# A transformer block's slot schedule: one values product deferred by a slot, odd maxima in a second PSUM bank

## The chip, the cores and the metric

The kernel runs on one core of one Trainium2 chip. The metric is the device time of one execution in microseconds (us), smaller is better. Engines are named as the profile names them: PE (TensorE matmul), PEld (TensorE weight load), DVE (VectorE), ACT (ScalarE), POOL (GpSimd), SP (SyncE, which issues most DMAs).

## What is computed

64 sequences of 128 tokens with 128 features attend to 77 keys of a context each (16 heads of depth 8); then a router sends each token to two of eight experts. Cut to what matters:

```python
x = x + tanh(g_xattn[0]) * xattn(_layernorm(x), ctx, ctx, wq, wk, wv)   # 16 heads, softmax over 77 keys
x = x + tanh(g_ffn[0]) * ffn(_layernorm(x), Wr, br, W1, b1, W2, b2)
# ffn: logits = x @ Wr + br; the best two experts of each token, gates = softmax over those two
#      h = relu(x @ W1[e] + b1[e]); out = sum of gates * (h @ W2[e] + b2[e])
```

## The kernel before

The work is cut by sequence (b = 0 to 63) and by group of four sequences (g = 0 to 15). Every engine runs its own list of instructions in order, and the lists are written out by hand: a loop over slots t = 0 to 103 (`slot(t)` of each engine, with u = t // 4 and r = t % 4) in which different sequences stand at different stages. In slot t the maxima of the scores are taken for sequence mx = t - 8, the scores, exponentials and value products for sc = t - 13, and the turning back and the residual of the attention for ob = t - 14. Between engines only semaphores order the work.

The steps of one sequence, four times each (h = 0 to 3, four heads at a time):

- `max_scores(b, h)` (L472, matmul at L482): PE writes scores of all queries into a PSUM bank; `head_max(b, h)` (L1023, L1028) on DVE takes the negated maximum over keys. From the fifth sequence on all four use the one bank `max_scores`, so a product waits until the maximum before it is taken (L477 to L479).
- `scores(b, h)` (L494, L503): scores with the maxima already subtracted, into two banks by turns; waits for the exponential two steps back. `exp_scores` (L740, L744) on ACT makes `probs`.
- `values(b, h)` (L507, L517): `probs` times values, into the bank `bank_oT`; `values(b, 0)` also waits until the bank was copied out for the sequence before. After the fourth, `output_rows(b)` on ACT (L734, L738) copies the bank to `oT`.
- `turn_o` (L521, L530) on PE turns `oT` back; `heads_normed` (L1041) on DVE divides by the sum, `add_attention` and `stats2_of` follow.

By r, once for each group, come `project_k` (r 0, L442), `turn_x1` (r 1, L448), `project_q` (r 2, L453), `project_v` (r 3, L458), `turn_x2` (r 3, L468) and `route` (r 0, L541), which puts router products into columns of the maxima's bank, where `make_logits` on DVE (L1062, L1067) reads them; the third maximum of an r 0 slot waits for that read (L480). `turn_max` (L486, L491) turns the maxima of two sequences. The queries go from `project_q` over ACT (`q_high`, L756) and DVE (`q_low`, L1020) through DRAM (`store_q`, then `stack_q`, L361, on SP) and come back stacked; the first maximum of the group, at r 0 two slots later, waits for them.

38 quads (four expert tiles of 128 rows each) are placed in slots 43 to 50, 55 to 62, 67 to 73, 75 and from 78 on. A quad has `hidden_part(q, 0)` and `(q, 1)` (L569, L591 to L593) in its slot, each into the bank `hidden_p`, which `relu` on ACT (L801, L810) must have read before the next one writes it; `rows_out` (L596, L605 and L607) in the slot after into the bank `y`; and `outputs` (L815, L819), the copy of `y` by ACT. From slot 81 on 16 dense units follow.

PE's slot order before, for what the prediction follows: `turn_max`, S0, M0, project, `hidden_part(q, 0)`, S1, M1, `turn_o`, `route`, `rows_out(q-1, 0)`, V0, S2, M2, `rows_out(q-1, 1)`, `turn_x1` or `project_v`, V1, S3, M3, V2, `hidden_part(q, 1)`, `turn_x2`, V3. (S, M and V are scores, maxima and values of h.) ACT's: copy of the turned maxima, `output_rows`, exp 0, `k_high` or `q_high`, relu of the first half, exp 1, `outputs`, exp 2, `turned_x1` or `v_columns`, exp 3, relu of the second half, `turned_x2`.

Of the kernel before, what the change touches and what calls it, by code (L numbers as in the profile page):

```python
# [18 lines left out]
MAX_LAG = 8  # L19
# [10 lines left out]
def clip(n, top):  # L30
    return max(0, min(n, top))


def flamingo_kernel(nc, x, ctx_t, g_xattn, g_ffn, w_att_t, w_router, b_router, w1, b1, w2, b2, out):
# [39 lines left out]
    t = 0  # L74
# [28 lines left out]
    with ExitStack() as stack:  # L103
# [171 lines left out]
        def active(s):  # L275
            return 0 <= s < B

        def group_on(g):
            return 0 <= g < NG
# [148 lines left out]
        def _(pe):  # L428
# [224 lines left out]
            def slot(t):  # L653
                u, r = t // NB, t % NB
                mx, sc, ob = t - MAX_LAG, t - SCORE_LAG, t - OUT_LAG
                for q in quads_at(t):
                    name_weights(q)
                if r == 0 and group_on(u - 3):
# [3 lines left out]
                if active(sc):  # L662
                    scores(sc, 0)
                if active(mx):
                    max_scores(mx, 0)
                if r == 0 and group_on(u - 1):
                    project_k(u - 1)
                if r == 2 and group_on(u - 1):
                    project_q(u - 1)
                for n in dense_at(t):  # L670
                    dense_units(n)
                for q in quads_at(t):
                    hidden_part(q, 0)
                if active(sc):
                    scores(sc, 1)
                if active(mx):
                    max_scores(mx, 1)
                if active(ob):
                    turn_o(ob, t)
                if r == 0 and group_on(u - 5):  # L680
                    route(u - 5, t)
                for q in quads_at(t - 1):
                    rows_out(q, 0)
                if active(sc):
                    values(sc, 0)
                    scores(sc, 2)
                if active(mx):
                    max_scores(mx, 2)
                for q in quads_at(t - 1):
                    rows_out(q, 1)  # L690
# [4 lines left out]
                if active(sc):  # L695
                    values(sc, 1)
                    scores(sc, 3)
                if active(mx):
# [12 lines left out]
                if active(sc):  # L711
                    values(sc, 3)

# [6 lines left out]
        def _(act):  # L720
# [139 lines left out]
            def slot(t):  # L860
# [20 lines left out]
                if t in (16, 17, 18):  # L881
                    b2_part(t - 16)
                if r == 0 and group_on(u - 3):
                    turned_max(u - 3, 1)
                if r == 2 and group_on(u - 2):
                    turned_max(u - 2, 0)
                if active(ob):
                    output_rows(ob)
                for q in quads_at(t - 2):
                    store_y(q)  # L890
                for n in dense_at(t):
                    dense_relu(n)
                if active(sc):
                    exp_scores(sc, 0)
                if r == 0 and group_on(u - 1):
                    k_high(u - 1)
                if r == 2 and group_on(u - 1):
                    q_high(u - 1)
                for q in quads_at(t):
                    name_biases(q)  # L900
                    relu(q, 0)
                if active(sc):
                    exp_scores(sc, 1)
                for q in quads_at(t - 1):
                    outputs(q)
                if active(sc):
                    exp_scores(sc, 2)
                if r == 1 and group_on(u - 1):
# [40 lines left out]
        def _(dve):  # L949
# [283 lines left out]
            def slot(t):  # L1233
# [21 lines left out]
                if r == 0 and group_on(u - 5):  # L1255
                    make_logits(u - 5)
                if active(ob):
                    heads_normed(ob)
                if active(mx):
                    head_max(mx, 2)  # L1260
                if active(t):
                    mean_var1(t)
                if active(ob):
                    add_attention(ob)
                    stats2_of(ob)
# [192 lines left out]
```

## Time and profile before

| | |
|---|---|
| time, median of 3 runs | 645.9 us (645.79 to 646.98) |
| span of the profiled execution | 693.9 us |
| PE busy | 579.1 us (83%) |
| DVE busy | 374.7 us (54%) |
| ACT busy | 363.7 us (52%) |
| POOL busy | 265.3 us (38%) |
| granted TensorE clock, mean | 0.925 of 2.4 GHz |

The profiled execution is longer than the timed runs, so a sum of its durations is made against 693.9 us. PE's matmuls are pipelined: a row's duration runs to its modelled end, and the next matmul may start before that, so what a product takes of PE's time is read from one start to the next. In the timeline a row has start, duration, engine, line, operation, out<-in and, in brackets, PE's idle time before it and what ended it. In the view of windows the first figure is the length, then the busy time of each engine with its number of instructions, the granted clock (1.00 is 2.4 GHz, 0.50 is 1.2 GHz), and DMA. In the view of waits the figures are total us, number of waits, longest. In the chain a row has start, us and what.

### The profile page before, as it was taken

Reading aid. Unit: us, or ns where it says so; the run is one execution under the profiler, and the core shown is the slowest. Engines: PE = TensorE matmul, PEld = TensorE weight load, DVE = VectorE, ACT = ScalarE, POOL = GpSimd, SP = SyncE. Lnnn points to the kernel's source line nnn. Section 1 sums busy time; section 2 is a strip of 40 time slices with the busy share of each in tenths; the row PEclk is TensorE's granted clock in tenths of the full one; section 3 lists DMA queues with packets and bytes.
Section 4 is the critical chain, followed back from the end, with each engine's and each line's share of the span. In section 5 each row is a group of like instructions: output and inputs, shape, how many; then the busy total and the mean of one; then the engine's idle time right before and its main releaser. Section 6 shows DMA issues by size and latency. Waiting matters only on the chain.

```text
span 693.9 us, 18476 instructions
## 1 busy us (share of the span) xinstructions
PE 579.1 (83%) x6201; PEld 412.4 (59%) x6213; DVE 374.7 (54%) x1361; ACT 363.7 (52%) x835; POOL 265.3 (38%) x281
## 2 busy tenths in 40 slices
PE   2459998989787999899789899788886788899877
PEld 0225555555455566666467667466664587778656
DVE  4455876688655765445765554665543331242354
ACT  5216765655455466666456656455555345456222
POOL 6020010100554002443544435544455255566660
PEclk9968998988788899999999999899999689999999
DMA  4445644544433376664676654553332245764221
GB/s 116 118 115 148 159 107 126 137 105 119 142 95 112 73 118 104 148 103 138 104 132 115 147 109 139 97 125 83 97 107 81 70 98 136 133 148 128 77 77 49
DMA packets 158121, 78.65 MB, mean 113 GB/s; under 512 B 85088, under 2 KB 153312, under 8 KB 158032
## 3 DMA queue, kind: packets, MB, share of 16 engines
q1 hardware_dynamic: 119760, 45.65, 30.4%
q0 software_dynamic: 7168, 14.69, 8.9%
q10 hardware_dynamic: 31104, 17.13, 8.9%
q8 instruction: 54, 0.88, 0.5%
q14 instruction: 35, 0.29, 0.2%
HBM read 30.72 MB, written 36.75 MB: 97 GB/s over the span
## 4 chain that ended last, share of the span: by engine, by line
PE 65%; issue 9%; DMA 7%; DVE 7%; ACT 7%; another core or an unknown queue 2%; POOL 1%; ACTq 1%; SPq 1%; DVEq 0%; POOLq 0%
PE y L607 11%; PE bank_oT L517 9%; PE scores L503 8%; PE max_scores L482 5%; DMA q_st<-q_dram 4%; PE hidden_p L591 4%; PE o L530 3%; PE hidden_p L592 3%; PE hidden_p L593 3%; DVE neg_max L1028 3%; ACT probs L744 2%; PE max_scores L541 2%; PE bank_oT L648 2%; ACT hidden L810 2%
## 5 line engine op out<-in xcount | busy, mean ns | idle before, releaser
L1028 DVE TENSOR_REDUCE neg_max<-max_scores 128x4 f32<-128x308 f32 x244 | 116.2, 476 | 158.7 <-PE max_scores L482 149.4
L744 ACT ACTIVATE probs<-scores 77x512 f32<-77x512 f32 x256 | 148.8, 596 | 69.9 <-PE scores L503 64.2
L1351 POOL DMA_INDIRECT xs_dram<-rows,at x112 | 110.1, 983 | 92.6 <-PE max_scores L482 57.4
L1366 POOL DMA_INDIRECT back<-ys_dram,at x112 | 107.8, 963 | 90.4 <-PE max_scores L482 35.9
L517 PE MATMUL bank_oT<-probs,v_cols 77*9 77x128 f32 x2048 | 110.0, 291 | 13.6 <-ACT probs L744 8.6
L503 PE MATMUL scores<-q_st,k_st 128*77 128x128 bf16 x1024 | 111.7, 236 | 0.1
L482 PE MATMUL max_scores<-k_st,q_st 128*128 128x308 bf16 x244 | 78.8, 323 | 34.9 <-DVE neg_max L1028 12.3
L503 PEld LDWEIGHTS scores<-q_st,k_st 128*77 128x77 bf16 x1024 | 76.5, 124 | 50.8 <-issue 43.7
L810 ACT ACTIVATE hidden<-hidden_p,b_cols 128x128 f32<-128x128 f32 x256 | 73.5, 369 | 54.3 <-PE hidden_p L593 43.3
L607 PE MATMUL y<-w_sb,hidden 128*128 x608 | 96.8, 299 | 0.0
L607 PEld LDWEIGHTS y<-w_sb,hidden 128*128 128x128 f32 x608 | 84.7, 201 | 2.7
L517 PEld LDWEIGHTS bank_oT<-probs,v_cols 77*9 77x9 f32 x2048 | 30.8, 89 | 59.8 <-issue 28.1
L591 PE MATMUL hidden_p<-xsT,w_sb 128*128 128x128 bf16 x256 | 53.5, 228 | 15.2 <-ACT hidden L810 10.7
L819 ACT COPY ys<-y 128x512 f32<-128x512 f32 x38 | 22.3, 588 | 82.1 <-PE y L607 66.0
L1312 POOL TENSOR_TENSOR rstd<-ve,power 128x4 f32<-128x4 f32 x16 | 17.7, 1107 | 114.2 <-DVE ve L996 114.2
L1306 POOL TENSOR_TENSOR rstd<-ve,power 128x4 f32<-128x4 f32 x16 | 16.4, 1027 | 113.3 <-DVE ve L969 90.8
L593 PE MATMUL hidden_p<-xsT,w_sb 128*128 128x128 bf16 x256 | 52.7, 222 | 0.3 <-issue 0.3
L592 PE MATMUL hidden_p<-xsT,w_lo 128*128 128x128 bf16 x256 | 52.6, 222 | 0.0
L482 PEld LDWEIGHTS max_scores<-k_st,q_st 128*128 128x128 bf16 x244 | 25.1, 103 | 45.6 <-DVE neg_max L1028 20.8
L738 ACT COPY oT<-bank_oT 128x512 f32<-128x512 f32 x64 | 37.6, 587 | 22.2 <-PE bank_oT L517 15.1
L530 PE MATMUL o<-ident,oT 128*128 128x128 f32 x256 | 43.2, 296 | 5.9 <-ACT oT L738 5.9
L591 PEld LDWEIGHTS hidden_p<-xsT,w_sb 128*128 x256 | 25.2, 99 | 32.1 <-issue 27.4
(144 smaller groups left out, 931.9 us busy)
## 6 DMA issues: line engine op xcount, KB each, us to landing
ys_dram<-ys ACTq DMA_DIRECT2D x38, 256.0 KB
q_st<-q_dram SPq DMA_DIRECT2D x16, 512.0 KB
k_st<-k_dram SPq DMA_DIRECT2D x64, 77.0 KB
xs_all<-x SPq DMA_DIRECT2D x16, 256.0 KB, 4.2
q_dram<-q_hl SPq DMA_DIRECT2D x16, 256.0 KB
xs_dram<-zeros_b ACTq DMA_DIRECT2D x16, 256.0 KB, 3.5
out<-xs_all SPq DMA_DIRECT2D x16, 256.0 KB
k_dram<-k_hl SPq DMA_DIRECT2D x48, 77.0 KB
```

The source lines that it names most:

```text
L482: mm(max_to(b, h)[:, 0:PER * KEYS], q_st[g % 3][:, h, seq_cut(b, S)], k_st[g % 3][:, h, b % NB, :, :].rearrange("p j k -> p (j k)"), start ...
L503: last = mm(score_bank[h % 2][0:KEYS, j * S:(j + 1) * S], k_st[g % 3][:, h, b % NB, j, :], q_st[g % 3][:, h, seq_cut(b, S)], start=True, s ...
L517: last = mm(oT_bank[ROWS * j:ROWS * j + VW, h * S:(h + 1) * S], v_cols[g % 3][:, b % NB, h * PER + j, :], probs[h][:, j * S:(j + 1) * S], ...
L591: mm(o, w_hi[:, at_w], tiles[:, 0, cut], start=True, stop=False, skip_group_check=True)
L592: mm(o, w1_lo[:, at_w], tiles[:, 0, cut], start=False, stop=False, skip_group_check=True)
L593: last = mm(o, w_hi[:, at_w], tiles[:, 1, cut], start=False, stop=True, skip_group_check=True)
L607: last = mm(o, hidden[:, (2 * q + t // 2) % 4, t % 2, m, :], w2_sb[:, bass.ds(w + m * 128, 128)], start=False, stop=(m == HC - 1), skip_gr ...
L744: nc.scalar.activation(probs[h][:], score_bank[h % 2][0:KEYS, :], ACT.Exp, scale=SCALE).then_inc(s_exp, 1)
L810: last = nc.scalar.activation(hidden[:, k % 4, i, m, :], of[:, j * 128:(j + 1) * 128], ACT.Relu, bias=b1_cols[:, bass.ds(held[q][2 * half ...
L1028: V.tensor_reduce(neg_max[:, i // 2, :, h, i % 2], max_to(b, h)[:, 0:PER * KEYS].rearrange("p (j k) -> p j k", j=PER), AXIS_X, ALU.max, ne ...
L1351: G.indirect_dma_start(out=xs_dram[c % 2], out_offset=bass.IndirectOffsetOnAxis(ap=at[k][c % 4][:, i:i + 1], axis=0), in_=rows[c % 2][:, i ...
L1366: G.indirect_dma_start(out=back[k][:, b % 16, :], out_offset=None, in_=ys_dram[c % 2][0:TILES[c] * 128, :], in_offset=bass.IndirectOffsetO ...
```

## The change

Three things. First, the fourth values product V3 moves from the end of its slot to the next slot, behind S0, M0 and S1 of the next sequence; `output_rows` and `turned_max` on ACT move behind exp 0, and `turn_o` behind V0. Second, the order of the rest: projections behind V3 and `turn_max`, M1 ahead of `hidden_part(q, 0)`, S2 ahead of `route` and M2 right behind it, S3 ahead of V1, `turn_x1` and `project_v` behind V1; ACT takes exp 1 ahead of the first relu and exp 2 ahead of `outputs`; DVE takes `heads_normed` behind the third maximum. Third, in slots without a quad the odd maxima (h = 1 and 3, from the fifth sequence on) go to the bank `hidden_p`, so an even and an odd maximum no longer wait for one another; waits keep the bank between maxima and quads.

```diff
+        def lent(b, h):
+            return h % 2 == 1 and b >= NB and not quads_at(b + MAX_LAG)
         def max_to(b, h):
-            return (max_bank, score_bank[0], score_bank[1], y_bank)[h] if b < NB else max_bank
+            if b < NB:
+                return (max_bank, score_bank[0], score_bank[1], y_bank)[h]
+            return hidden_bank if lent(b, h) else max_bank
+        def max_before(b, h):   # number of the maximum last taken in the same bank
...
 # max_scores
-                n = HG * b + h + 1 - (HG if b < NB else 1)
-                if n > 0:
-                    pe.wait_ge(s_max, n)
+                if max_before(b, h) > 0:
+                    pe.wait_ge(s_max, max_before(b, h))
+                if lent(b, h) and quads_before(b + MAX_LAG):
+                    pe.wait_ge(s_relu, 2 * quads_before(b + MAX_LAG))
 # hidden_part
+                if half == 0 and lent_before(QUAD_AT[q]):
+                    pe.wait_ge(s_max, lent_before(QUAD_AT[q]))
 # PE's slot, the order after
+ scores(sc, 0); max_scores(mx, 0); scores(sc, 1); values(ob, 3); turn_max; project_k or project_q;
+ max_scores(mx, 1); dense_units; hidden_part(q, 0); scores(sc, 2); route; max_scores(mx, 2);
+ values(sc, 0); turn_o(ob); rows_out(q-1, 0); scores(sc, 3); values(sc, 1); turn_x1 or project_v;
+ rows_out(q-1, 1); max_scores(mx, 3); values(sc, 2); dense_out; hidden_part(q, 1); turn_x2; ranks
 # ACT's slot, the order after
+ exp 0; store_y; output_rows(ob); turned_max; k_high or q_high; dense_relu; exp 1; relu(q, 0);
+ exp 2; outputs(q-1); turned_x1 or v_columns; exp 3; relu(q, 1); rows_high, turned_x2
 # DVE's slot
-                if active(ob):
-                    heads_normed(ob)
                 head_max(mx, 2); mean_var1(t)
+                if active(ob):
+                    heads_normed(ob)
```

(The orders of PE and ACT are written here as lists; the diff has them as moved blocks.)

## Rows read from the trace of the kernel before

**Rows 1.** The page: span, and the chain that ended last, shares by engine.
```profile
span 693.9 us, 18476 instructions
...
PE 65%; issue 9%; DMA 7%; DVE 7%; ACT 7%; another core or an unknown queue 2%; POOL 1%; ACTq 1%; SPq 1%; DVEq 0%; POOLq 0%
```

**Rows 2.** Windows by stage: early attention, quads, and the end.
```profile
57.74:115.76 58.02, 52.58 (x676) 32.49 (x674) 43.06 (x159) 40.38 (x76) 5.05 (x5) 1.00 0.53 142
116.62:182.00 65.38, 58.48 (x651) 35.77 (x648) 50.76 (x190) 36.39 (x70) 9.31 (x9) 0.85 0.46 117
182.00:243.04 61.04, 50.49 (x517) 31.66 (x516) 37.67 (x142) 29.16 (x57) 24.59 (x25) 0.78 0.40 105
243.04:317.96 74.92, 68.75 (x845) 51.84 (x841) 38.96 (x142) 47.37 (x124) 24.77 (x25) 1.00 0.66 123
455.57:534.70 79.13, 69.17 (x872) 51.71 (x869) 41.03 (x153) 46.24 (x121) 37.33 (x38) 0.99 0.37 94
534.70:693.90 159.20, 132.04 (x1120) 110.65 (x1128) 51.74 (x184) 66.56 (x174) 81.13 (x84) 0.92 0.43 102
```

**Rows 3.** Waits of PE: first two rows from 48.95:182, the others from 243.04:534.70.
```profile
PE max_scores L482 <- DVE neg_max L1028: 5.8, 15, 0.9
PE max_scores L482 <- DMA q_st<-q_dram: 1.9, 4, 1.1
...
PE hidden_p L591 <- ACT hidden L810: 7.5, 11, 1.2
...
PE bank_oT L517 <- ACT probs L744: 6.2, 17, 0.5
PE group L442 <- ACT xT L777: 4.1, 4, 1.1
```

**Rows 4.** Timeline of ACT and PE in a slot with a quad.
```profile
297.13 0.59 ACT L819 COPY ys<-y 128x512 f32<-128x512 f32 x1 [3.34 <-PE y L607]
297.61 1.08 ACT L744 ACTIVATE probs<-scores 77x512 f32<-77x512 f32 x2
...
298.26 0.41 PE L517 MATMUL bank_oT<-probs,v_cols 77*9 77x128 f32 x8 [0.35 <-ACT probs L744]
```

**Rows 5.** Timeline of PE in a slot without a quad, r 1.
```profile
93.76 0.29 PE L482 MATMUL max_scores<-k_st,q_st 128*128 128x308 bf16 x1
93.89 0.39 PE L503 MATMUL scores<-q_st,k_st 128*77 128x128 bf16 x4
94.63 0.30 PE L482 MATMUL max_scores<-k_st,q_st 128*128 128x308 bf16 x1 [0.35 <-DVE neg_max L1028]
...
98.34 0.41 PE L517 MATMUL bank_oT<-probs,v_cols 77*9 77x128 f32 x8 [0.22 <-ACT probs L744]
98.68 0.24 PE L491 MATMUL o<-ident_b,nm_hl 128*64 128x128 bf16 x1
```

**Rows 6.** Timeline around the router's products, r 0: PE, then DVE.
```profile
89.96 1.03 PE L541 MATMUL max_scores<-wr_sb,xT 128*128 128x8 f32 x8 [0.46 <-issue]
...
91.03 0.19 DVE L1067 TENSOR_TENSOR logits<-max_scores,br_sb 128x32 f32<-128x32 f32 x1 [0.79 <-PE max_scores L541]
```

**Rows 7.** Chain of waits, 98 to 112 us: the way of the queries.
```profile
99.40 0.86 PE group L453 x2
...
102.17 2.70 DMA q_dram<-q_hl
...
104.89 5.85 DMA q_st<-q_dram
...
110.78 0.32 PE max_scores L482
```

**Rows 8.** Windows: four slots, one r 1 slot of them, a later r 1 slot.
```profile
87.26:109.30 22.04, 20.05 (x256) 12.46 (x255) 16.71 (x62) 14.53 (x29) 2.02 (x3) 1.00 0.52 137
...
93.51:98.85 5.34, 4.60 (x65) 2.76 (x62) 4.42 (x18) 3.34 (x6) 0.07 (x1) 1.00 0.52 116
...
116.62:123.93 7.31, 6.95 (x66) 4.35 (x62) 4.51 (x18) 3.51 (x6) 0.08 (x1) 0.59 0.49 94
```

More of the change, by code:

```diff
@@ L292, in ranks_before, with lent_before @@
             return len([c for c in range(NC) if RANKED[c] < s])
+        def lent(b, h):
+            return h % 2 == 1 and b >= NB and not quads_at(b + MAX_LAG)
         def max_to(b, h):
-            return (max_bank, score_bank[0], score_bank[1], y_bank)[h] if b < NB else max_bank
+            if b < NB:
+                return (max_bank, score_bank[0], score_bank[1], y_bank)[h]
+            return hidden_bank if lent(b, h) else max_bank
+        def max_before(b, h):
+            if b < NB:
+                return HG * (b - 1) + h + 1
+            n = HG * b + h - 1
+            while n >= HG * NB and lent(n // HG, n % HG) != lent(b, h):
+                n -= 1
+            if n >= HG * NB:
+                return n + 1
+            return 0 if lent(b, h) else HG * (NB - 1) + 1
+        def lent_before(s):
+            return max([HG * b + h + 1 for b in range(clip(s - MAX_LAG, B)) for h in range(HG) if lent(b, h)], default=0)
         def dense_before(s):
@@ L657, in slot @@
                     name_weights(q)
+                if active(sc):
+                    scores(sc, 0)
+                if active(mx):
+                    max_scores(mx, 0)
+                if active(sc):
+                    scores(sc, 1)
+                if active(ob):
+                    values(ob, 3)
                 if r == 0 and group_on(u - 3):
@@ L661, in slot @@
                     turn_max(u - 2, 0)
[L662 to L665, printed above, removed]
                 if r == 0 and group_on(u - 1):
@@ L669, in slot @@
                     project_q(u - 1)
+                if active(mx):
+                    max_scores(mx, 1)
                 for n in dense_at(t):
@@ L674, in slot @@
                 if active(sc):
-                    scores(sc, 1)
+                    scores(sc, 2)
+                if r == 0 and group_on(u - 5):
+                    route(u - 5, t)
                 if active(mx):
-                    max_scores(mx, 1)
+                    max_scores(mx, 2)
+                if active(sc):
+                    values(sc, 0)
                 if active(ob):
                     turn_o(ob, t)
-                if r == 0 and group_on(u - 5):
-                    route(u - 5, t)
                 for q in quads_at(t - 1):
@@ L684, in slot @@
                 if active(sc):
[L685 to L690, printed above, removed]
+                    scores(sc, 3)
+                    values(sc, 1)
                 if r == 1 and group_on(u - 1):
@@ L694, in slot @@
                     project_v(u - 1)
-                if active(sc):
-                    values(sc, 1)
-                    scores(sc, 3)
+                for q in quads_at(t - 1):
+                    rows_out(q, 1)
                 if active(mx):
@@ L710, in slot @@
                         ranks(c)
-                if active(sc):
-                    values(sc, 3)
             pe.wait_ge(s_wa, 16)
@@ L882, in slot @@
                     b2_part(t - 16)
+                if active(sc):
+                    exp_scores(sc, 0)
+                for q in quads_at(t - 2):
+                    store_y(q)
+                if active(ob):
+                    output_rows(ob)
                 if r == 0 and group_on(u - 3):
@@ L886, in slot @@
                     turned_max(u - 2, 0)
-                if active(ob):
[L888 to L894, printed above, removed]
                 if r == 0 and group_on(u - 1):
@@ L898, in slot @@
                     q_high(u - 1)
+                for n in dense_at(t):
+                    dense_relu(n)
+                if active(sc):
+                    exp_scores(sc, 1)
                 for q in quads_at(t):
@@ L902, in slot @@
                 if active(sc):
-                    exp_scores(sc, 1)
+                    exp_scores(sc, 2)
                 for q in quads_at(t - 1):
                     outputs(q)
-                if active(sc):
-                    exp_scores(sc, 2)
                 if r == 1 and group_on(u - 1):
@@ L1262, in slot @@
                     mean_var1(t)
+                if active(ob):
+                    heads_normed(ob)
                 if active(ob):
```

1 line of the change is left out of this document (removed).

## The prediction

> **What bounds the kernel now.** I read the page first, then windows by stage, then PE's waits, then single slots. The chain that ended last lies on PE for 65% of the 693.9 us, with 9% "issue" (PE waiting for nothing that the profile shows) and only 7% each on DMA, DVE and ACT [rows 1]. The windows by stage say that this PE is nearly full wherever quads run: 68.75 of 74.92 us at full clock, 69.17 of 79.13 us in the last quad stage [rows 2]. From 534.7 us on no attention runs, every moved call is inactive there, and the relative order of what is left on each engine stays: these 159.2 us [rows 2] are not touched. The change can act on about 486 us of slots, through PE's idle time, through what PE redoes at half clock, and through nothing else: it adds no product and removes none.
>
> There are three kinds of slot. In slots with a quad PE's holes are `hidden_part` waiting for the relu of the half before (7.5 us, 11 waits), a values product waiting for its exponential (6.2 us, 17) and `project_k` waiting for `turned_x2` (4.1 us, 4) [rows 3]. In early slots without a quad the holes are maxima waiting for DVE (5.8 us in 15 waits) and, at r 0, the first maximum waiting for the stacked queries (1.9 us in 4) [rows 3]. In late slots without a quad, 182 to 243 us, PE is busy 50.49 of 61.04 us and the granted clock is 0.78 [rows 2]: half clock costs there more than any one wait.
>
> **Small prices, from start to start at full clock.** S is 93.51 to 93.76, 0.25 us; M 93.76 to 93.89, 0.13; V 98.34 to 98.68, 0.34; `turn_max` 98.68 to 98.85, 0.17 [rows 5, 8].
>
> **Slots with a quad: values.** V2 waits 0.35 us in the shown slot because ACT takes `outputs` first, which itself waits for `rows_out` (3.34 us idle), and only then exp 2 and exp 3 [rows 4]. After the change exp 2 stands ahead of `outputs`, so V2 has its input long before; V3, whose exponential now sits behind `outputs`, is a slot later, behind S0, M0 and S1. Of the 6.2 us I take 5.0 (bounds 0 and 6.2; most of the 17 waits are of this kind).
>
> **Slots with a quad: the hidden bank.** After the second hidden part PE now has S0, M0, S1, V3, M1 ahead of the next first hidden part; before it had V3, S0, M0. The relu's end does not move, so the hole is filled by S1 + M1 = 0.38 us: 11 waits by 0.38 is 4.2 us; the last slots have no maxima, there it is 0.25. I take 4.0 (bounds 2.8 and 4.2). M1 must now wait for the first maximum, one DVE round behind M0, but S1 and V3 (0.59 us) stand between, and the relu that PE waits for ends later still.
>
> **Slots with a quad: `project_k`.** It waits for the end of an ACT queue that is not reordered there. Only S1 moves ahead of the hole: 4 x 0.25 = 1.0 us gained.
>
> **A new wait behind the router.** M2 now follows `route` directly, and at r 0 it waits until `make_logits` has read the bank. The router's products end at 90.99, DVE reads them from 91.03 to 91.22 [rows 6]; before, V0 and S2 (0.59 us) lay there and hid it. V0, `turn_o` and all behind M2 wait with it. That is about 0.3 us (bounds 0 and 0.35) in each r 0 slot that has both: 7 of them from slot 43 on, 2.1 us lost.
>
> **Slots without a quad.** With two banks M1 no longer waits for a DVE round (0.35 us in the shown r 1 slot) and V3's 0.22 us goes [rows 5]. Of four slots' 22.04 us PE is idle 1.99 [rows 8]; 0.46 of it is before the router's products, which still wait for the second maximum [rows 6]. Against the gain stand new waits, which the trace does not show and which I bound by a walk along both queues. V3 now comes after S1, exp 0 precedes `output_rows` on ACT, so V0 waits for a copy that starts some 1.1 us into the slot (0 to 0.2 us at r 1 and r 3). `turn_x1` and `project_v` move behind V1, their ACT copies stand ahead of exp 3, and S1 of the next slot and V3 wait for exp 3: 0 to 0.4 us. `turn_x2` has only M3 and V2 (0.47 us) between it and `project_v`, whose copy of 0.6 us it waits for: 0 to 0.36 us. Together up to 1.5 us in four slots, as much as can be gained. From slot 43 on there are two such fours: I take 2.0 us for the banks less 1.5 for the new waits, 0.5 gained. Slots 35 to 42: another 0.5. `heads_normed` moves behind the third maximum at no cost: `turn_o` is later too, DVE is busy 4.42 of 5.34 us [rows 8], and what follows it (`add_attention`, the second layer norm) has slots of slack.
>
> **The queries' way.** From `project_q` (ends 100.26) over ACT, DVE and two DMAs of 2.70 and 5.85 us the first maximum starts at 110.78 [rows 7]. It was late there: PE waited up to 1.1 us [rows 3]. The change puts S1, V3 and `turn_max` (0.76 us) between M0 and `project_q`. In the period from M0 of one group to M0 of the next the DMA way stays as it is and the rest gets 0.76 us longer, plus 0.3 behind the router, less the removed waits (0.35 + 0.22 and the like in two slots). I take +0.2 us for each of the five groups of slots 13 to 34, 1.0 us lost (bounds -0.5 and +4.0). `store_max` stands ahead of `store_q` in SP's queue, and its input is now two ACT copies later (two take 1.08 us [rows 4]); but `turn_max` and its copy still precede `project_q` and `q_high` on both engines, so SP has it issued first. `project_k` is later by the same 0.76 us; its stacked keys are needed a whole group later.
>
> **Sum.** -5.0 - 4.0 - 1.0 + 2.1 - 1.0 + 1.0 = -7.9 us of 693.9, 1.14%. The timed median is 645.9, 0.931 of the profiled span; I scale the sum by that: -7.4, **638.5 us**. With each bound taken on its side it runs from 632 (-14.4 us) to 648 (+2.7 us).
>
> **Rivals.**
>
> *The clock follows (B).* Between 116.6 and 243 us the clock is 0.85 and 0.78 [rows 2], which is 19.6 and 26.9 us at 1.2 GHz. An r 1 slot that is mostly at 1.2 GHz (0.59 on the mean, 6.0 of its us) takes 7.31 instead of 5.34 us [rows 8]: 0.33 us for each us at the low level, 15 us in all. If half of it goes because PE stands still less often, 7.6 us more come off: 631. All of it: 624. For it: the low stretches lie only in slots without a quad. Against it: from 57.7 to 115.8 us PE is idle 9% in the same short holes and the clock is 1.00 [rows 2], so short holes are not what brought it down. The Trainium skill (TensorE: Matmul & The Clock Gate, "A second HAM failure mode: psum-queue depth-cycling") says that cycling through PSUM banks makes PE idle briefly between groups so often that the clock swings between its levels; by that rule the second bank would give this rival. The trace of 57.7 to 115.8 us disagrees.
>
> *The queries' wait grows and takes the clock (D), slower.* Slots 16 to 44 have eight first maxima that wait for stacked queries. Filled holes elsewhere do not shorten the DMA way; they only bring PE to M0 sooner, where it then stands in one piece, some 2 us instead of up to 1.1. After the group with the 1.1 us wait (M0 at 110.78) the clock was low in the next slot [rows 7, 8], for the first time since 57.7 us [rows 2]. Price: 8 x 0.76 = 6.1 us, and 1.97 us for each added low stretch (7.31 - 5.34). With four of them it is 14.0 us against the 8.4 gained from slot 43 on: +5.6 us, scaled 651; it turns to slower from the second added stretch on. The Trainium skill (the same page, "HAM oscillation — how this bites in real kernels") says that bursts of products with a DMA wait between them start each burst at the low clock; by that rule it would be so here. The trace bears it out once for sure, so this is no small case.
>
> *Round trips only change their place (C).* The new waits of 1.5 us in four slots and behind the router come at their upper bounds, and in quad slots ACT (47.37 of 74.92 us busy [rows 2]) gives exp 3 and the relus back what exp 2 gained: about 645.5.
>
> **How the numbers follow.** The forecast has 0.46, B 0.18, C 0.13, D 0.23. The range from 624 to 652 holds B with all of its clock and D with four stretches. About 0.2% (1.3 us) is what a measurement of this kernel can tell from no change. Faster is the forecast and B, 0.64; same is C, 0.13; slower is D, 0.23.
>
> **What would show it.** Right: in the quad stages the waits of L517 for the exponential nearly gone and those of L591 and L442 shorter by 0.25 to 0.38 us each, quad slots some 0.4 us shorter; M2 waiting about 0.3 us for the logits at r 0; maxima in slots without a quad not waiting for DVE. The forecast falls if the stages before 243 us change by more than 3 us either way: down with a clock of 0.95 is B, up with M0 waiting 2 us and a clock below 0.8 is D. If the quad stages don't get shorter, it is C.

## The result and the profile after

The changed kernel takes 656.4 us (median of 20 runs, 646.9 to 666.7) against 646.9 us for the kernel before in the same session (20 runs, 638.2 to 656.3): ratio 1.0137, 95% interval 1.0105 to 1.0169. It is slower; the forecast was 638.5 us and its range ended at 652.

One remark on reading: each profile is of one execution. The trace ahead of the prediction (693.9 us) is longer than any timed run, so after (span 650.6 us) is compared here with a second trace of the unchanged kernel (`before_again`, span 645.2 us, time 646.97 us). These two differ by 5.4 us, the timed medians by 9.5, since the trace of after is of one of its shorter executions. The traces of `warm`, `early_both`, `early_q` and `lent_only` are of executions 4 us or more above the medians of their runs, and their stage lengths are upper values.

From the page of after: the granted clock in 40 slices of the span, and the chain that ended last.

```profile
PEclk9969889697877959999979999999999979999999
...
PE 63%; DMA 13%; DVE 7%; ACT 6%; issue 5%; SPq 3%; POOL 2%; ACTq 1%; DVEq 0%; POOLq 0%
```

The same of the second trace of the kernel before.

```profile
PEclk9976999899888799999998999999999979999999
...
PE 62%; DVE 9%; DMA 8%; issue 7%; ACT 7%; SPq 3%; POOL 2%; ACTq 1%; DVEq 0%; POOLq 0%
```

On the chain DMA went from 8% to 13% and DVE from 9% to 7% (before, in the first trace: [rows 1]). The low slices lie mostly among the first 15 of 40, ahead of the quads. Now the span cut in three: from the first S0 of slot 13 to slot 43 ("early", no quads), from there to the last S0 of slot 76 ("quads"), and the rest ("tail"). The columns are those of [rows 2]; first the kernel before (second trace), then after.

```profile
49.20:228.80 179.60, 162.49 (x1909) 99.41 (x1908) 135.93 (x506) 110.04 (x211) 39.11 (x38) 0.90 0.51 129
228.80:510.40 281.60, 254.93 (x3123) 187.16 (x3122) 163.50 (x605) 172.12 (x438) 128.23 (x131) 0.99 0.58 119
510.40:645.20 134.80, 121.84 (x1122) 104.63 (x1128) 51.91 (x184) 66.11 (x173) 81.30 (x85) 0.96 0.51 120
```

```profile
48.10:243.30 195.20, 176.76 (x1900) 108.09 (x1899) 138.49 (x505) 106.84 (x211) 38.68 (x38) 0.84 0.45 119
243.30:517.10 273.80, 252.91 (x3124) 186.77 (x3124) 168.01 (x607) 169.33 (x436) 127.98 (x131) 0.99 0.56 122
517.10:650.60 133.50, 120.69 (x1126) 104.35 (x1136) 52.68 (x187) 66.40 (x174) 82.06 (x85) 0.96 0.51 122
```

Early is 15.6 us longer, quads 7.8 us shorter, the tail 1.3 us shorter. In early, PE's idle time is 195.20 - 176.76 = 18.4 us against 179.60 - 162.49 = 17.1: it hardly changed. PE's busy time grew by 14.3 us with the same products. The granted clock goes with it: 0.84 against 0.90 is, counted in the clock records, 63.2 against 35.0 us at 1.2 GHz, 28.2 us more. If PE gets half as far in a us at half clock, half of these, 14.1 us, is what the low clock costs. That is an estimate; the 14.3 us of busy time are measured and fit it.

Where the idle time of early went, from PE's waits in these stretches (total us, number, longest): the kernel before, then after.

```profile
PE max_scores L482 <- DVE neg_max L1028: 8.8, 19, 1.2
PE max_scores L482 <- DMA q_st<-q_dram: 2.2, 3, 1.2
```

```profile
PE max_scores L501 <- DMA q_st<-q_dram: 10.3, 7, 2.5
PE max_scores L501 <- DVE logits L1089: 2.3, 6, 0.4
...
PE max_scores L501 <- DVE neg_max L1050: 1.2, 2, 0.8
```

The second bank took away nearly all waits for DVE (8.8 to 1.2 us), and the wait of the first maximum for the stacked queries took the same time back (2.2 to 10.3 us). Waits for the router's logits (2.3 us in six) are new. Most of the holes that were filled came together in one place.

### The profile page after: what moved, and what is told of

It is laid out like the page before. It is cut to its first block, busy times and chain, and to the rows that moved or that the text cites. A ratio compares the mean times of both kernels' runs of the same rounds, so it can differ in the third digit from the quotient of the medians.

```text
span 650.6 us, 18493 instructions
## 1 busy us (share of the span) xinstructions
PE 568.4 (87%) x6201; PEld 408.0 (63%) x6213; DVE 377.6 (58%) x1361; ACT 357.5 (55%) x835; POOL 265.0 (41%) x281
## 4 chain that ended last, share of the span: by engine, by line
PE 63%; DMA 13%; DVE 7%; ACT 6%; issue 5%; SPq 3%; POOL 2%; ACTq 1%; DVEq 0%; POOLq 0%
PE y L628 12%; PE bank_oT L536 9%; DMA q_st<-q_dram 7%; PE scores L522 6%; PE o L549 5%; DMA q_dram<-q_hl 4%; PE max_scores L501 3%; PE hidden_p L612 3%; PE max_scores L560 2%; PE hidden_p L613 2%; PE bank_oT L669 2%; PE group L460 2%; DVE neg_max L1050 2%; PE o L669 2%; PE hidden_p L614 2%
## 5 line engine op out<-in xcount | busy, mean ns | idle before, releaser
L1050 DVE TENSOR_REDUCE neg_max<-max_scores 128x4 f32<-128x308 f32 x166 | 78.9, 475 | 88.2 <-PE max_scores L501 87.2
L522 PE MATMUL scores<-q_st,k_st 128*77 128x128 bf16 x1024 | 108.9, 236 | 5.7 <-ACT probs L766 4.9
L522 PEld LDWEIGHTS scores<-q_st,k_st 128*77 128x77 bf16 x1024 | 88.7, 127 | 27.7 <-issue 12.6
L628 PE MATMUL y<-w_sb,hidden 128*128 x608 | 93.2, 292 | 0.0
L501 PE MATMUL max_scores<-k_st,q_st 128*128 128x308 bf16 x166 | 53.4, 322 | 34.3 <-DMA q_st<-q_dram 22.3
L628 PEld LDWEIGHTS y<-w_sb,hidden 128*128 128x128 f32 x608 | 82.0, 196 | 1.8
L841 ACT COPY ys<-y 128x512 f32<-128x512 f32 x38 | 22.3, 587 | 86.2 <-PE y L628 86.2
L612 PE MATMUL hidden_p<-xsT,w_sb 128*128 128x128 bf16 x256 | 50.9, 225 | 6.4 <-ACT hidden L832 6.0
L1050 DVE TENSOR_REDUCE neg_max<-hidden_p 128x4 f32<-128x308 f32 x78 | 36.6, 470 | 26.1 <-PE hidden_p L501 25.9
L614 PE MATMUL hidden_p<-xsT,w_sb 128*128 128x128 bf16 x256 | 49.9, 221 | 0.0
L613 PE MATMUL hidden_p<-xsT,w_lo 128*128 128x128 bf16 x256 | 49.8, 221 | 0.0
L501 PEld LDWEIGHTS max_scores<-k_st,q_st 128*128 128x128 bf16 x166 | 17.3, 104 | 43.5 <-DMA q_st<-q_dram 24.2
```

Source lines behind the costliest of these rows:

```text
L522: last = mm(score_bank[h % 2][0:KEYS, j * S:(j + 1) * S], k_st[g % 3][:, h, b % NB, j, :], q_st[g % 3][:, h, seq_cut(b, S)], start=True, s ...
L612: mm(o, w_hi[:, at_w], tiles[:, 0, cut], start=True, stop=False, skip_group_check=True)
L614: last = mm(o, w_hi[:, at_w], tiles[:, 1, cut], start=False, stop=True, skip_group_check=True)
L628: last = mm(o, hidden[:, (2 * q + t // 2) % 4, t % 2, m, :], w2_sb[:, bass.ds(w + m * 128, 128)], start=False, stop=(m == HC - 1), skip_gr ...
L1050: V.tensor_reduce(neg_max[:, i // 2, :, h, i % 2], max_to(b, h)[:, 0:PER * KEYS].rearrange("p (j k) -> p j k", j=PER), AXIS_X, ALU.max, ne ...
```

## The place of the loss: one period of a group

Group after group, M0 waits for queries that `project_q` started two slots earlier. One period is the way from `project_q` to M0 and the stretch from M0 to the next `project_q`. For the groups 4 to 9 the way is 11.9 us on the mean before and 11.8 after. These are the stretches from M0 to the next `project_q`, columns as above: first before (second trace), then after.

```profile
112.81:124.99 12.18, 11.25 (x129) 7.25 (x129) 8.76 (x32) 5.86 (x12) 0.46 (x1) 0.86 0.42 82
135.49:147.70 12.21, 10.05 (x128) 6.44 (x129) 10.47 (x41) 6.31 (x12) 0.46 (x1) 1.00 0.44 92
160.70:172.92 12.22, 11.25 (x128) 7.25 (x129) 10.34 (x39) 6.22 (x13) 0.46 (x1) 0.86 0.31 74
184.87:198.47 13.60, 12.73 (x131) 8.00 (x130) 8.76 (x32) 6.84 (x15) 10.47 (x11) 0.75 0.51 131
209.34:222.87 13.53, 12.47 (x129) 7.86 (x130) 10.56 (x41) 6.12 (x12) 1.38 (x2) 0.75 0.40 66
```

```profile
113.44:129.32 15.88, 15.14 (x141) 9.43 (x141) 9.80 (x34) 6.46 (x14) 0.90 (x1) 0.68 0.35 71
139.94:155.79 15.85, 15.12 (x141) 9.24 (x141) 11.91 (x46) 6.02 (x14) 1.01 (x1) 0.68 0.32 69
167.20:183.04 15.84, 15.12 (x142) 9.19 (x142) 12.12 (x43) 6.97 (x15) 1.54 (x1) 0.68 0.36 89
195.94:210.77 14.83, 13.88 (x141) 8.33 (x141) 9.84 (x34) 6.54 (x15) 8.63 (x9) 0.77 0.44 108
221.69:237.55 15.86, 15.13 (x141) 9.23 (x141) 11.91 (x46) 6.01 (x13) 1.37 (x2) 0.68 0.33 56
```

The mean goes from 12.75 to 15.65 us, 2.9 us more for each group, against the 0.2 that the prediction took. A row has 141 products or 142 instead of 128 to 131: S1, V3 and `turn_max`, 13 products, which the change put between M0 and `project_q`, 0.76 us by the prediction's prices at full clock. PE's idle time fell, from 1.20 to 0.77 us. So busy time grew by 3.3 us, and 2.6 of them are neither idle nor new products. They go with the clock: 0.70 against 0.84 on the mean, or 9.5 against 4.1 us of a stretch at 1.2 GHz in the clock records. With half of that time taken off, as above, the stretches would be 10.9 and 10.7 us at full clock. By this estimate they are 0.2 us apart, which is just the prediction's term.

The timeline of PE in one of these stretches of after (start, duration, idle time before it in brackets):

```profile
139.94 0.30 PE L501 MATMUL max_scores<-k_st,q_st 128*128 128x308 bf16 x1 [1.02 <-DMA q_st<-q_dram]
140.08 0.39 PE L522 MATMUL scores<-q_st,k_st 128*77 128x128 bf16 x4
140.39 0.41 PE L536 MATMUL bank_oT<-probs,v_cols 77*9 77x128 f32 x8
...
142.39 1.06 PE L560 MATMUL max_scores<-wr_sb,xT 128*128 128x8 f32 x8 [0.35 <-DVE neg_max L1050]
143.83 0.29 PE L501 MATMUL max_scores<-k_st,q_st 128*128 128x308 bf16 x1 [0.38 <-DVE logits L1089]
...
145.90 0.62 PE L536 MATMUL bank_oT<-probs,v_cols 77*9 77x128 f32 x8
146.45 0.65 PE L522 MATMUL scores<-q_st,k_st 128*77 128x128 bf16 x4
```

S1 and V3 stand behind M0, the wait behind the router is 0.38 us, and eight values products take 0.41 us at first and 0.62 from 145.90 on (to the next start 0.55 us, where 0.34 was the price at full clock). The clock has fallen, between 5 and 6 us behind M0 and some 2 us behind the wait for the router, and stays low to the end of the stretch.

## Experiments

Theory W: the queries' way and the stretch behind M0 set the period of the early slots, and the wait at M0 takes the clock. Against it stand other places of the loss: the new short waits of the order (theory T of the expectations), the second bank, the deferred V3. Ratios are to the kernel before on the same chip; early and quads are stage lengths as cut above, with the granted clock of early.

| kernel | ratio | 95% | early us | clock | quads us |
|---|---|---|---|---|---|
| before (second trace) | 1 | | 179.6 | 0.90 | 281.6 |
| after | 1.0137 | 1.0105 to 1.0169 | 195.2 | 0.84 | 273.8 |
| `early_q` | 1.0128 | 1.0065 to 1.0191 | 188.9 | 0.87 | 282.5 |
| `early_both` | 1.0080 | 1.0038 to 1.0122 | 197.4 | 0.84 | 284.6 |
| `lent_only` | 0.9919 | 0.9878 to 0.9960 | 180.9 | 0.92 | 283.4 |
| `no_lent` | 1.0448 | 1.0385 to 1.0512 | 208.5 | 0.82 | 281.8 |
| `warm` | 1.0086 | 1.0041 to 1.0131 | 196.1 | 0.85 | 278.0 |
| `v3_back` | 1.0180 | 1.0122 to 1.0237 | 191.8 | 0.87 | 280.8 |
| `late_q` | 1.0150 | 1.0112 to 1.0189 | 190.9 | 0.89 | 280.2 |
| `hybrid` | 0.9861 | 0.9797 to 0.9924 | 181.4 | 0.90 | 269.3 |
| `split_before` | 0.9906 | 0.9874 to 0.9937 | 178.7 | 0.91 | 280.1 |
| `split_after` | 0.9899 | 0.9810 to 0.9988 | 182.2 | 0.91 | 280.6 |
| `split_lent` | 0.9776 | 0.9721 to 0.9831 | 168.8 | 0.94 | 277.4 |
| `hybrid_split` | 0.9646 | 0.9604 to 0.9688 | 170.5 | 0.98 | 269.3 |

A stage length is of one execution, but the granted clock is on record for every timed run. Its mean over the whole kernel, in the runs that the ratios use, is 0.957 for the kernel before (session of `lent_only`), 0.939 for after, 0.960 for `lent_only`, 0.918 for `no_lent` and 0.974 for `hybrid_split`: the order in which the traces put them.

**The unchanged kernel once more** (`before_again`, no edit).

> The kernel before once more, for a trace whose length is that of the timed runs (the first one has a span of 693.9 us, the median is 645.9). Both theories expect a span of 638 to 652 us with the early slots (13 to 34) at 130 us or a little less and the quad slots shorter than in the first trace. If the quad slots (43 to 50, 55 to 62) come out at 72 to 73 us each, as in the changed kernel, the gain read there between the first two traces is none; if at 75 to 76, it is real.

Its span is 645.2 us. The tail, 159.2 us in the first trace [rows 2], is 134.8 here and 133.5 after: most of the first trace's extra time lay there and in the last slots of early, and has nothing to do with the change.

**The projection of the queries back to its old place** (`early_q`, in the changed kernel).

```diff
 # PE
   max_scores(mx, 0)
+  project_q at r 2
   scores(sc, 1); values(ob, 3); turn_max; project_k
-  project_q at r 2
 # ACT: q_high right behind exp 0; DVE: q_low ahead of the second maximum
 # SP: store_q ahead of store_max
```

> The changed kernel with the queries' projection and its copies moved ahead again: project_q right behind the first maximum on PE, q_high behind exp 0 on ACT, q_low ahead of the second maximum on DVE, store_q ahead of store_max on SP; all else as changed. Theory W (the loss is the wait of the first maximum at r 0 for the stacked queries, and the clock that falls behind it): that wait gets 0.8 to 1.2 us shorter, r 0 slots without a quad fall from a mean of 8.3 us to about 7.2, the low clock stretches shrink, 646 us or less, ratio to before 0.990 to 1.002. Theory T (the loss is the new short waits spread over all slots without a quad: S1 behind exp 3, M2 behind the logits, V0 behind the copy): ratio stays at 1.010 to 1.016.

1.0128: W's forecast missed, the slots with r 0 stayed at 8.3 us on the mean (6.1 before). The edit was not clean: on SP, `store_q` now stood ahead of `store_max`, and `stack_q` behind the stack of the turned maxima, which waits for `store_max` to land. In one group `store_q` is issued at 209.82 us, the maxima are stored at 210.74 and stacked at 213.44, and the queries are stacked only at 214.18. On the mean of the groups 4 to 9 the way got 1.0 us longer than in after (12.8 against 11.8). What PE gave, SP took.

**The same without SP, S1 and V3 behind the projections** (`early_both`, in the changed kernel).

```diff
 # PE
-  max_scores(mx, 0); scores(sc, 1); values(ob, 3); turn_max; project_k or project_q; max_scores(mx, 1)
+  max_scores(mx, 0); turn_max; project_k or project_q; scores(sc, 1); values(ob, 3); max_scores(mx, 1)
 # ACT
-  store_y; output_rows(ob); turned_max; k_high or q_high
+  turned_max; k_high or q_high; store_y; output_rows(ob)
```

> The changed kernel with turn_max and the projections ahead of S1 and V3 on PE (behind S0 and M0, as before the change), and their ACT copies ahead of output_rows; SP's order is left alone, which early_q had turned round and so put the queries' load behind the landing of the maxima. Theory W (lateness of the queries): their way starts 0.6 us earlier in each group, r 0 slots without a quad fall from 8.3 to about 7.6 us, ratio to before 1.002 to 1.009. Rival T (the rest of the order makes r 0 slots long, whatever the projection's place): r 0 slots stay at 8.1 us or more, ratio 1.010 to 1.017.

1.0080; the median of all its runs, 655.2 us, is hardly below after's 656.4. S1 and V3, 0.59 of the 0.76 us, are out of the way of `project_q` here; `turn_max` still stands ahead of it. By the two ratios that is worth 0.6%, by their intervals 0 to 1.1%: the smaller part of what the new order costs in these slots (2.7%, see `hybrid`). This is not settled any finer.

**The second bank alone** (`lent_only`, in the kernel before) **and the new order alone** (`no_lent`, in the changed kernel).

```diff
 # lent_only: lent, max_to, max_before, lent_before and their waits of the change, with the orders of before
 # no_lent
         def lent(b, h):
-            return h % 2 == 1 and b >= NB and not quads_at(b + MAX_LAG)
+            return False
```

> The kernel before with the third part of the change alone: odd maxima in the bank hidden_p in slots without a quad, order of all slots as before. Theory W: the waits of maxima for DVE go (some 0.3 us in most slots), but in slots 13 to 42 the first maximum at r 0 waits longer for the queries by the same amount: ratio 0.996 to 1.004. Theory T: the bank is the good part of the change and the order the bad one: ratio 0.985 to 0.995.

> The changed kernel with its third part undone: all maxima in their one bank, new order kept. Theory W: the order alone is the loss and the second bank a gain of about 1% even here: ratio 1.015 to 1.026. Rival: the bank shared with the quads is part of the loss (a maximum waiting for a relu and a quad for a maximum): ratio 1.000 to 1.012.

The bank alone gains 0.8%; the order alone loses 4.5%, more than expected. Within the new order the bank gives back 3% (1.0448 to 1.0137): M1 stands there close behind M0, and with one bank it waits for DVE each time.

The wait rows of early tell the two apart from after: first `no_lent`, then `lent_only`.

```profile
PE max_scores L501 <- DVE neg_max L1050: 15.9, 37, 1.1
...
PE max_scores L501 <- DMA q_st<-q_dram: 0.3, 1, 0.3
```

```profile
PE max_scores L501 <- DMA q_st<-q_dram: 11.0, 7, 2.0
```

`lent_only` decides much. Its first maxima wait for the queries as long as after's (11.0 us in 7 against 10.3 in 7), its PE is idle even longer in early (180.86 - 158.56 = 22.3 us against 18.4), and yet early takes 14 us less, since its busy time is 158.6 instead of 176.8 us. Its stretches from M0 to `project_q`:

```profile
112.72:123.85 11.13, 9.98 (x128) 6.29 (x129) 8.56 (x32) 5.70 (x12) 0.45 (x1) 1.00 0.34 73
135.75:148.55 12.80, 11.25 (x128) 7.37 (x129) 10.46 (x41) 5.52 (x10) 0.46 (x1) 0.88 0.32 66
161.66:175.82 14.16, 13.94 (x129) 9.00 (x130) 10.55 (x39) 5.87 (x12) 0.47 (x1) 0.64 0.32 73
188.16:200.16 12.00, 11.16 (x128) 7.20 (x129) 8.75 (x32) 5.84 (x12) 9.46 (x10) 0.86 0.43 111
211.27:223.25 11.98, 10.03 (x128) 6.34 (x129) 10.36 (x41) 5.42 (x10) 1.99 (x3) 1.00 0.27 56
```

Two of the five run at full clock throughout, right behind a wait for the queries:

```profile
112.72 0.30 PE L501 MATMUL max_scores<-k_st,q_st 128*128 128x308 bf16 x1 [1.54 <-DMA q_st<-q_dram]
...
211.27 0.30 PE L501 MATMUL max_scores<-k_st,q_st 128*128 128x308 bf16 x1 [1.06 <-DMA q_st<-q_dram]
```

So that wait by itself does not take the clock; half of theory W falls. The Trainium skill (TensorE: Matmul & The Clock Gate, "HAM oscillation — how this bites in real kernels") says that a burst of products behind a DMA wait starts at the low clock. Its DMA waits are of some 3 to 5 us; those here, of 1 to 2.5 us, are shorter and not its case, so the prediction's use of it for rival D did not hold.

`no_lent` says it from the other side. Its first maxima hardly wait for the queries (0.3 us in all of early), PE's longest idle time there is 1.1 us, and its clock is the lowest of all, 0.82. In its stretches behind M0 the clock is full at first and falls 3.8 to 5.1 us behind M0, in all five groups 4 to 8; here group 8, whose M0 did not wait at all:

```profile
235.70:239.50 3.80, 3.15 (x32) 2.28 (x30) 2.34 (x6) 3.17 (x8) 0.53 (x1) 1.00 0.02 4
239.50:253.20 13.70, 12.60 (x103) 7.28 (x103) 9.05 (x36) 3.93 (x7) 0.72 (x1) 0.50 0.42 62
```

In after it falls 4.2 to 5.7 us behind M0 in four of the same five groups. What stands there in both kernels is the router: PE waits 0.35 us, runs its products of 8 columns for 1.06 us, and in the new order waits again, 0.38 us, for the logits. The kernel before (second trace) has falls at this place too (4.6 to 5.5 us behind M0, in four of the five), but not the second wait. That this passage takes the clock is not shown; no run moved it by itself.

**The wait filled with products** (`warm`, in the changed kernel; eight products on zero data into the maxima's bank ahead of M0, added work without effect on the output).

```diff
+            def keep_busy(b, n):
+                pe.wait_ge(s_max, HG * b - 1)
+                for _ in range(n):
+                    mm(max_bank[:], ident_b[:], zeros_b[:], start=True, stop=True, skip_group_check=True)
 # max_scores
+                if b % NB == 0 and h == 0 and 8 <= b < 36:
+                    keep_busy(b, 8)
```

> The changed kernel with eight products of 512 columns, of no use, in the maxima's bank just ahead of the first maximum of groups 2 to 8, so that PE does not stand still while it waits for the queries (8 x 0.22 = 1.7 us at 2.4 GHz, 3.4 us at 1.2 GHz; the outputs are untouched). Theory W with the clock as its larger part: the granted clock of slots 13 to 42 rises from about 0.84 to 0.95 or more and 6 to 10 us come off against the changed kernel, ratio to before 0.998 to 1.006. If the clock is the smaller part or not the cause: the clock stays below 0.88 or the time does not follow it, ratio 1.010 to 1.025.

First PE's wait for the queries in early, then the window of early.

```profile
PE max_scores L508 <- DMA q_st<-q_dram: 1.6, 2, 1.5
```

```profile
49.01:245.10 196.09, 185.50 (x1949) 111.92 (x1955) 138.03 (x505) 106.94 (x211) 40.01 (x38) 0.85 0.47 117
```

The idle time at M0 is gone (10.3 to 1.6 us) and the clock is 0.85 where it was 0.84, 58.5 us at the low level against 63.2. The time, 1.0086, lies between the two forecasts, and its interval overlaps with after's. Whether products on zeros count for the clock as others do, no run here shows; the run points the same way as `lent_only` and `no_lent`: not the idle time at M0 by itself.

**V3 back into its own slot** (`v3_back`, in the changed kernel).

```diff
 # PE
   scores(sc, 1)
-  values(ob, 3)
...
   ranks
+  values(sc, 3)
```

> The changed kernel with one part undone: the fourth values product back at the end of its own slot, all other orders as changed. Theory W: one product (0.34 us) less between the first maximum and the queries' projection, 8 x 0.34 = 2.7 us and one or two low stretches less: ratio 1.003 to 1.011. Rival V (putting V3 off is itself the loss, through the copy of bank_oT and V0 that wait for it): ratio 0.995 or less. If V3 put off is what gained in the quad slots, these lengthen by 0.2 us or more each.

1.0180, no better than after and outside both forecasts: early is 3.4 us shorter in the trace, quads are 7.0 us longer at a clock of 0.97 (slots 43 to 50 and 55 to 62 take 74.1 and 74.6 us against 72.3 and 72.7). Putting V3 off is not what makes the change slower.

**`project_q` later in the old order** (`late_q`, in the kernel before, slots without a quad).

```diff
-  project_q; hidden_part(q, 0); scores(sc, 1); max_scores(mx, 1)
+  hidden_part(q, 0); scores(sc, 1); max_scores(mx, 1); project_q
```

> The kernel before with one product moved and nothing else: in slots without a quad the queries' projection stands behind S1 and M1 instead of ahead of them, which makes it some 0.8 us later (M1 waits there for DVE). Theory W: the way of the queries to the next first maximum starts that much later in eight groups, and the clock falls oftener: 4 to 9 us, ratio 1.004 to 1.014. Rival T (the place of the projection does not matter, the loss of the change lies in its other moves): ratio 0.997 to 1.003.

1.0150 from one product moved; but two things are mixed in it. The slots with r 2 got longer (72.5 against 64.1 us in 11), since `project_q` no longer covers M1's wait for DVE, and the slots with r 0 (59.7 against 54.8 in 9), which is the later queries. Only the second is W's. It says that the place of `project_q` costs in the old order too, not how much.

**The new order only in slots with a quad** (`hybrid`: the second bank everywhere, orders of before in slots without a quad, V3 put off only out of a slot with one).

```diff
+        def new(t):
+            return bool(quads_at(t))
 # PE, ACT, DVE
+                if new(t):
+                    (the order after; V3 of the slot before only if new(t - 1))
+                else:
+                    (V3 of the slot before if new(t - 1); the order before)
```

> Slots with a quad in the new order (V3 put off only out of these), slots without one in the order of before, odd maxima in the second bank as changed. Theory W: the new order gains only where PE has quads to do (8 us of the first comparison) and loses only where the queries are late, so the gains of lent_only (5 us) and of the quad slots add up: ratio 0.974 to 0.988. Rival: the gain in the quad slots hangs on the order of the slots around them, or is given back where the kinds of slot meet: ratio 0.988 to 1.000.

0.9861: against after 2.7% faster. Early is back at 181.4 us. Quads are 269.3, 4.5 us shorter than in after, nearly all of it in the slots without a quad between them; the slots 43 to 50 and 55 to 62 take 72.5 and 72.8 us, as in after (72.3 and 72.7), against 74.7 and 76.8 in the second trace of the kernel before. The new order loses in the slots without a quad and gains in those with one.

**The queries' load cut in two** (`split_after`, `split_before`, `split_lent`: in after, before and `lent_only`). The first half carries the group's first two sequences, so M0 waits for half of the bytes, and r 2, two slots later, for the rest.

```diff
-                sp.dma_start(q_st[g % 3][:], q_dram[g % 2].rearrange("(h p) t n -> (p t) h n", h=HG)
-                             ).then_inc(s_qst[g % 3], 16)
+                for half, done in enumerate((s_qst, s_qst2)):
+                    n = slice(half * 2 * S, (half + 1) * 2 * S)
+                    sp.dma_start(q_st[g % 3][:, :, n], stacked[:, :, n]).then_inc(done[g % 3], 16)
 # max_scores
+                if b % NB == 2 and h == 0:
+                    pe.wait_ge(s_qst2[g % 3], 16 * (g // 3 + 1))
```

> The changed kernel with the load of the stacked queries cut in two, the first two sequences of the group first; the first maximum at r 0 waits for that half alone (2.5 to 3.5 us instead of 4 to 6 from its issue). Theory W (wait of the first maximum, and the clock behind it): that wait gets 1.5 us or more shorter, r 0 slots without a quad fall from 8.3 us to 7 or less, and 8 to 14 us come off: ratio to before 0.993 to 1.003. Rival T (the loss is the order of PE in slots without a quad and the waits it makes there, whatever the queries do): the time that comes off at M0 is given back within the slot, ratio 1.009 to 1.016.

> The kernel before with the stacked queries loaded in two halves, nothing else. Theory W: the kernel before was already held by this wait in slots 16 to 42, by 0.5 to 1.6 us a group: ratio 0.985 to 0.995; less than the same cut gave the changed kernel (1.0137 to 0.9899), as its wait is shorter. Rival: before had slack there and the cut does nothing: ratio 0.996 to 1.003.

> The kernel before with the second bank for odd maxima (lent_only) and the stacked queries loaded in two halves. Theory W: what the second bank frees was swallowed by the queries' wait at r 0 (68.7 us in nine r 0 slots of lent_only against 54.8 before); with the wait cut it shows: ratio 0.975 to 0.987. Rival T: the wait only moves to the second half of the queries or to the maxima's turn: ratio 0.988 to 0.997, no better than lent_only.

From the pages, DMA issues with count, KB each and median us to landing: first after, then `split_after`.

```profile
q_st<-q_dram SPq DMA_DIRECT2D x16, 512.0 KB, 4.4
```

```profile
q_st<-q_dram SPq DMA_DIRECT2D x32, 256.0 KB, 3.4
```

1 us less of landing turns the changed kernel from 1.0137 to 0.9899, below the kernel before and better than W asked; early goes from 195.2 to 182.2 us and its clock from 0.84 to 0.91 (over the whole kernel, mean of the runs that the ratio uses, from 0.939 to 0.951). The same cut is worth 0.9% in the old order and 1.4% on top of the bank. So this half of W stands: the queries' way holds the early slots wherever M0 waits for it (in `no_lent` it does not). But the cut does not act through idle time alone. Of the 13.0 us that early lost against after, 11.4 are busy time (176.8 to 165.4 us) and 1.6 idle; against `lent_only` it was 4.5 busy and 7.5 idle. A shorter wait went with a higher clock here, and why is open.

**Both** (`hybrid_split`: `hybrid` with the load cut in two).

> The parts that gained, together: second bank for odd maxima, new order in slots with a quad alone, stacked queries in two halves. Theory W: hybrid against lent_only gave 0.6%, split_lent against lent_only 1.4%; they act in different slots and add up: ratio 0.965 to 0.975. Rival: a later wait takes over (the products of the quads waiting for their scattered rows, the end of the kernel): ratio 0.976 or more, no better than split_lent.

0.9646, 622.8 us (620.1 to 626.5), faster than both kernels. From `split_lent` (0.9776) it differs by the new order in slots with a quad alone, and the intervals are apart: there that order gains 1.3%. Its waits for the queries in early, then the window of early:

```profile
PE max_scores L510 <- DMA q_st<-q_dram: 5.9, 6, 1.8
```

```profile
46.20:216.80 170.60, 150.82 (x1909) 92.41 (x1908) 134.11 (x508) 109.97 (x211) 39.83 (x38) 0.98 0.54 136
```

Six waits of up to 1.8 us are left, and the clock of early is 0.98. Against `hybrid` (8.6 us in six waits, clock 0.90) early is 10.9 us shorter, all of it busy time.

## Why the prediction was wrong

**Right: slots with a quad.** Forecast from slot 43 on was -8.4 us, measured -7.8 in this pair of traces. The size is of this pair: other kernels with the new order have 278 to 285 us in quads, at clocks of 0.95 to 0.97. The sign holds, by `hybrid_split` against `split_lent`. PE's waits there, the kernel before (second trace; the first is [rows 3]) and after:

```profile
PE hidden_p L591 <- ACT hidden L810: 7.3, 11, 0.8
PE bank_oT L517 <- ACT probs L744: 6.7, 19, 0.5
...
PE group L442 <- ACT xT L777: 2.6, 3, 1.0
```

```profile
PE max_scores L501 <- DVE logits L1089: 2.6, 7, 0.4
PE group L460 <- ACT xT L799: 2.5, 3, 0.8
PE scores L522 <- ACT probs L766: 2.1, 5, 1.1
PE hidden_p L612 <- ACT hidden L832: 2.0, 5, 0.7
PE group L486 <- ACT v_cols L792: 1.4, 2, 0.7
PE hidden_p L501 <- ACT hidden L832: 1.0, 2, 0.5
...
PE bank_oT L536 <- ACT probs L766: 0.2, 1, 0.2
```

- Values: -6.5 us (6.7 to 0.2), taken -5.0.
- Hidden bank: -5.3, of which 1.0 comes back where a lent maximum waits for the relu; net -4.3, taken -4.0.
- `project_k`: -0.1, taken -1.0. S1 in front did not move its hole.
- Behind the router: seven waits, 2.6 us, taken seven of 0.3.
- The bounded new waits are there: S1 for exp 3 (2.1 us) and `turn_x2` for `project_v`'s copy (1.4 us), together 3.5 us, set against the gain of the banks. Their longest, 1.1 and 0.7 us, are over the bounds of 0.4 and 0.36.

PE's idle time gives 5.8 of the 7.8 us; the other 2.0 are busy time, which the prediction had not in its sum. So the mechanisms were right, and that the sum came so close is partly luck.

**Right: the tail**, 134.8 and 133.5 us.

**Right: slots without a quad, in PE's idle time.** The waits for DVE went and others came, 17.1 to 18.4 us in early (+1.3); the prediction's terms for slots 13 to 42 gave +0.5 (0.5 gained, 1.0 lost).

**Wrong: "the queries' way".** The step took +0.2 us per group, 1.0 us in all, with bounds of -0.5 and +4.0; measured are 2.9 us per group and 15.6 over early. The rows' count of products confirms the 13 that it priced at 0.76 us, and at full clock the estimate above gives its +0.2. What the step left out is that these products, and all behind them, run at whatever clock is granted: it summed at full clock in a stage whose clock was 0.78 to 0.85 [rows 2], and kept every change of clock for the rivals. 14.3 of the 15.6 us are busy time, with 28.2 us more at 1.2 GHz. The bounds were too narrow by nearly this term. One reading in this step was wrong without consequence: the 1.08 us of [rows 4] are of two exponentials, not of two copies.

**Rival D** gave the sign, the place and about the time (651). The wait at M0 grew as it said (2.2 to 10.3 us). Its chain did not hold as written: it let this wait take the clock, and `no_lent`, `lent_only` and `hybrid_split` speak against that, and `warm` as far as products on zeros count. So its sign came in part by luck. Its price of 0.33 us per us at the low level was low as well; the rows of early show 14.3 us of busy time for 28.2 us, 0.5. **Rival B** asked for the opposite, a clock that follows filled holes; the bank alone gave 0.92 for 0.90, the new order took it to 0.84.

**Open.** Why the clock stays low for 9.5 us of a stretch in the new order, and for 4.1 us in the old, is not settled. Excluded as the single cause are the idle time at M0, the second bank, the deferred V3 and, to within 1.1%, the place of `project_q`. What is shown is that the loss is in the order of the slots without a quad as a whole (`hybrid`); its wait behind the router, where the clock falls, was not tried by itself. Nor is it settled why the clock rose when the load was cut in two.

## What to carry to other kernels

Where a loop hangs on a round trip through DMA, cut its period into the way and the stretch back to the next start: holes filled on the way come back as one wait, and what is put into the stretch back lengthens every period. Price an order for each kind of slot, at the clock that the stage has and with a term for a change of it, and try it there alone; the same order gained in one kind and lost in the other. A load that is waited for can be cut by first need, which here was worth more than the whole reorder.

## What was not expected of the hardware

- The clock of one and the same stretch of products differs from group to group in one execution: 1.00, 0.88, 0.64, 0.86 and 1.00 in `lent_only`, with 128 or 129 products each.
- Long idle times are not needed for a low clock: in `no_lent`, where PE's longest idle time in early was 1.1 us, the clock of early was 0.82; in `lent_only`, where it was 2.0 us, 0.92.
- Half the bytes of the queries' load land only 1.0 us sooner (3.4 instead of 4.4 us).
- Two executions of the unchanged kernel had spans of 693.9 and 645.2 us; a single profiled execution that is far from the timed median shows stages (here the tail, 159.2 against 134.8 us) that are not typical.
